# First attention of a four-stage transformer kernel: the row maxima are turned through the weighted sum's PSUM bank and spread by VectorE

## The reference, cut to what matters

```
q, k, v = split_heads(lat @ Wq, kv_input @ Wkv)      # 16 heads of 64; kv_input = [context | latents]
dots = jnp.einsum('bhid,bhjd->bhij', q, k) * scale
attn = jax.nn.softmax(dots, axis=-1)
out = jnp.einsum('bhij,bhjd->bhid', attn, v)
x = x + out.transpose(0, 2, 1, 3).reshape(b, m, heads * dim_head) @ Wout
```

## Time and profile before

| | |
|---|---|
| median of 3 runs | 777.03 us (776.41 to 777.33) |
| the profiled execution | 778.1 us, of which the span of the trace is 776.2 |
| PE busy | 694.8 us, 90% of the span |
| VectorE busy | 472.0 us, 61% |
| ScalarE busy | 394.4 us, 51% |
| GpSimd busy | 378.5 us, 49% |
| granted TensorE clock, mean | 0.955 |

### The profile page before, as it was taken

How to read it: one execution, slowest core, us unless ns; L and a number is a source line. 1 busy time by engine, 2 the same in 40 slices (tenths; PEclk the granted TensorE clock), 3 DMA queues, 4 the chain that set the end, 5 groups by cost and what they waited for, 6 DMA issues and landing times. The chain is left out here.

```text
span 776.2 us, 13776 instructions
## 1 busy us (share of the span) xinstructions
PE 694.8 (90%) x4714; PEld 421.3 (54%) x4714; DVE 472.0 (61%) x966; ACT 394.4 (51%) x676; POOL 378.5 (49%) x362
## 2 busy tenths in 40 slices
PE   4899999999999999999999999997899378559991
PEld 3654555545556546545545545557799134336661
DVE  4735474775776676578468558475343459856553
ACT  4575664564655555555465464434464255234440
POOL 7164373464454565543475455444333403766552
PEclk9999999999999999999999999999999599659997
DMA  9999999999000000000030003310210700123325
GB/s 247 182 185 185 177 188 107 3 4 4 1 1 1 2 15 1 1 1 2 2 122 2 1 1 81 124 45 12 73 43 25 223 2 11 46 69 90 85 64 179
DMA packets 109866, 50.60 MB, mean 65 GB/s; under 512 B 44804, under 2 KB 103048, under 8 KB 109800
## 3 DMA queue, kind: packets, MB, share of 16 engines
q1 hardware_dynamic: 106280, 42.46, 40.7%
q0 software_dynamic: 3520, 7.27, 2.8%
HBM read 20.07 MB, written 29.64 MB: 64 GB/s over the span
## 5 line engine op out<-in xcount | busy, mean ns | idle before, releaser
L873 ACT ACTIVATE PT<-PSUM 128x1024 f32<-128x1024 f32 x128 | 128.7, 1025 | 131.4 <-PE PSUM L1636 131.1
L692 POOL TENSOR_TENSOR PSUMS<-PT 128x1024 f32<-128x1024 f32 x32 | 76.1, 2377 | 204.8 <-ACT PT L873 166.2
L692 POOL TENSOR_TENSOR PSUMS<-PSUMS,PT 128x1024 f32<-128x1024 f32 x62 | 150.5, 2427 | 16.7 <-ACT PT L873 9.8
L1261 DVE TENSOR_REDUCE TOPS<-PSUM 128x2 f32<-128x1024 f32 x128 | 151.5, 1219 | 7.6 <-PE PSUM L1605 7.0
L1668 PE MATMUL PSUM<-PT,BIG 128*64 128x512 f32 x512 | 130.6, 611 | 0.0
L1216 DVE TENSOR_TENSOR SIL<-SIL,PSUM 128x256 f32<-128x256 f32 (+1 forms) x62 | 32.2, 519 | 61.7 <-ACT SIL L785 61.7
L1251 DVE TENSOR_TENSOR KL<-PSUM,KH 128x512 fp32r<-128x512 f32 x32 | 22.1, 690 | 68.8 <-ACT KH L846 68.6
L1605 PE MATMUL PSUM<-KH,QH 64*128 64x512 f32 x256 | 58.5, 454 | 2.6 <-DVE QL L1254 2.6
L785 ACT ACTIVATE SIL<-PSUM 128x256 f32<-128x256 f32 (+1 forms) x62 | 28.7, 463 | 57.7 <-PE PSUM L1470 34.7
L1668 PEld LDWEIGHTS PSUM<-PT,BIG 128*64 128x64 f32 x512 | 28.4, 135 | 53.0 <-issue 51.6
L1605 PEld LDWEIGHTS PSUM<-KH,QH 64*128 64x128 f32 x256 | 24.4, 185 | 58.3 <-DVE TOPS L1261 24.7
(11 more groups left out here) (257 smaller groups left out, 1347.2 us busy)
## 6 DMA issues: line engine op xcount, KB each, us to landing
lists_d<-EMPTY SPq DMA_DIRECT2D x3, 2730.0 KB, 39.5
lists_b<-EMPTY SPq DMA_DIRECT2D x3, 2470.0 KB, 35.0
lists_d<-EMPTY SPq DMA_DIRECT2D x1, 2665.0 KB, 37.0
XG<-lists_d SPq DMA_DIRECT2D x39, 65.0 KB, 1.9
lists_b<-EMPTY SPq DMA_DIRECT2D x1, 2405.0 KB, 18.0
BIG<-in_L_ffn_w SPq DMA_DIRECT2D x1, 2048.0 KB, 8.5
W2ALL<-in_L_ffn_w SPq DMA_DIRECT2D x4, 512.0 KB, 6.3
PT<-results_d SPq DMA_DIRECT2D x8, 256.0 KB, 4.8
```

The lines of the kernel that those rows point to most:

```text
L692: pool.tensor_tensor(PSUMS[:, i % 2], PTT[:, i % 2, 0] if kt == 1 else PSUMS[:, i % 2], PTT[:, i % 2, kt], ALU.add).then_inc(s_ps, 1)
L873: act.activation(PTT[:, i % 2, kt], PSUM[:, place:place + 2, :], ACT.Exp, scale=DH ** -0.5).then_inc(s_exp, 1)
L1261: dve.tensor_reduce(TOPS[:, c, 0, :], PSUM[:, place:place + 2, :], AX.X, ALU.max).then_inc(s_max, 1)
```

## The change

The turned maxima go to bank 6, `mt` is no taker any more (so the round robin shifts for all steps behind it), VectorE's reduction becomes a step of its own (`row_max`, `rm`) ahead of `P0`, and the four ScalarE copies become one VectorE product, in VectorE's queue at the place of `mt`, that is ahead of `O1`.

```diff
-        TAKES_BANKS = {"values", "context_values", "qk", "top", "max_turn", "scores", ...}
+        TAKES_BANKS = {"values", "context_values", "qk", "top", "scores", ...}
...
-            "E A B PC CA0 C CA1 O0 ADD CS V qk p0 p1 t0 s0 t1 p2 t2 D s1 t3 p3 t4 P0 P2 s2 s3 rows mt O1 OUT "
+            "E A B PC CA0 C CA1 O0 ADD CS V qk p0 p1 t0 s0 t1 p2 t2 D s1 t3 p3 t4 rm P0 P2 s2 s3 rows mt O1 OUT "
...
-        order += first_top[4:] + [("max_turn", 0), ("context_kept", 1), ("counters", 0)]
+        order += first_top[4:] + [("row_max", 0), ("context_kept", 1), ("max_turn", 0), ("counters", 0)]
...
# ScalarE
-                elif name == "max_turn":
-                    act.wait_ge(s_topt, a + 1)
-                    if a >= GROUP:
-                        act.wait_ge(s_sc, context_of(a // GROUP - 1))
-                    if a == 0:
-                        act.wait_ge(*CONST.at(0, "own"))
-                    for t in range(TPB):
-                        last = act.activation(TOPROW[:, a % GROUP, t * P:(t + 1) * P], PSUM[:, place, 0:P], ACT.Copy,
-                                              scale=OWN_TILE[:, t:t + 1])
-                    last.then_inc(s_toprow, 1)
...
# VectorE
-                elif name == "max_turn":
+                elif name == "row_max":
                     dve.wait_ge(s_max, TOPS_OF * (a + 1))
...
+                elif name == "max_turn":
+                    dve.wait_ge(s_topt, a + 1)
+                    if a == 0:
+                        dve.wait_ge(*CONST.at(0, "own"))
+                    if a >= GROUP:
+                        dve.wait_ge(s_sc, context_of(a // GROUP - 1))
+                    dve.tensor_tensor(TOPROW[:, a % GROUP, :].rearrange("p (t n) -> p t n", t=TPB),
+                                      PSUM[:, 6, 0:P].unsqueeze(1).broadcast_to([P, TPB, P]),
+                                      OWN_TILE[:, :].unsqueeze(2).broadcast_to([P, TPB, P]), ALU.mult).then_inc(s_toprow, 1)
...
# TensorE
                 elif name == "max_turn":
                     pe.wait_ge(s_comb, a + 1)
-                    pe.transpose(PSUM[:, place, 0:P], TOPT[:, :], IDENT[:, :]).then_inc(s_topt, 1)
-                    release(mine, (s_toprow, a + 1))
+                    claim(6)
+                    pe.transpose(PSUM[:, 6, 0:P], TOPT[:, :], IDENT[:, :]).then_inc(s_topt, 1)
+                    free[6] = s_toprow, a + 1
...
                         pe.wait_ge(s_v, (b + 1) * KT)
-                        if i:
-                            free[6] = s_ot, i
                         claim(6)
```

More of the change, by code:

```diff
@@ L313, in build @@
         s_cadd = sem("c_added")
-        TAKES_BANKS = {"values", "context_values", "qk", "top", "max_turn", "scores", "context_scores", "context_sums", "spread", "out", "a_turn", "r0_turn", "r0_logits", "r0_run"}
+        TAKES_BANKS = {"values", "context_values", "qk", "top", "scores", "context_scores", "context_sums", "spread", "out", "a_turn", "r0_turn", "r0_logits", "r0_run"}
         ITERATION = (
-            "E A B PC CA0 C CA1 O0 ADD CS V qk p0 p1 t0 s0 t1 p2 t2 D s1 t3 p3 t4 P0 P2 s2 s3 rows mt O1 OUT "
+            "E A B PC CA0 C CA1 O0 ADD CS V qk p0 p1 t0 s0 t1 p2 t2 D s1 t3 p3 t4 rm P0 P2 s2 s3 rows mt O1 OUT "
             "O2 O3").split()
@@ L378, in build @@
                     order.append(("scores", (i, int(at[1]))))
-                elif at in ("qk", "mt") and i + 1 < ALL:
-                    order.append(("qk" if at == "qk" else "max_turn", i + 1))
+                elif at in ("qk", "rm", "mt") and i + 1 < ALL:
+                    order.append(({"qk": "qk", "rm": "row_max", "mt": "max_turn"}[at], i + 1))
                 elif at[0] == "t" and i + 1 < ALL:
```

## The result

The changed kernel took 795.43 us (median of 4 runs, 793.12 to 797.65) beside 777.18 us for the kernel before on the same chip: ratio 1.0229, 95% interval 1.0191 to 1.0266. It is slower, as forecast, but by 18 us and not by 11: 788.3 us had been predicted, with a range up to 792.0. Run again in another comparison it took 791.71 us (6 runs, 1.0191, 1.0158 to 1.0224). The ten executions lie between 791.37 and 797.65. The profiled one took 795.24 us with a span of 793.5, against 778.1 and 776.2 before.

The account below looks back on a forecast made before the run. TensorE, busy 90% of the span, was taken as the bound, so only its waits count. 6.1 + 1.15 + 1.6 + 3.6 + 1.2 - 0.84 - 1.1 - 0.5 = +11.3 on the median 777.03 gave 788.3 us; range 781.9 to 792.

Parts of the forecast that it names:

- The reciprocals' delay: Seven iterations: three reciprocals queue behind the product; in iteration 9 they end 3.54 us after the turn starts, before 1.26.
- L1287 held by GpSimd: VectorE product with two SBUF inputs, held by GpSimd's additions; iterations 9, 17 and 25 lose 2.03 each, 6.1 us.
- the cast in iterations 16 and 24: Router slot step on VectorE, held by GpSimd's second addition until 5.23 us after the turn starts; +1.8 twice, 3.6 us.
- the exponential at the loop's end: Last group's context sums, banks 2 and 3, wait for exponentials of s3 ending at 506.64: +1.2 us.
- the table's row of predicted steps: Extra time per loop iteration, turn to turn: from 0.43 to 2.03 in nine iterations, -2.4 in the others, loop 10.1 us.
- iteration 30: Step behind the turn of iteration 29, with the router's steps between L1287 and KL: +0.78 us.
- The gains: TOPROW waits gone in iterations 5, 13, 21 (0.84), seven plain iterations of 0.16 (1.1), context sums (0.5): 2.4 us.
- the 0.5 for the context sums: A smaller gap ahead of the context sums, estimated at 0.07 in seven iterations: gain of 0.5 us.
- the rivals: L1287 and slots unheld: 781.9 (0.12); only slots unheld: 784.7 (0.12); reciprocals' delay hidden: 774.6 (0.03); product held: 820 (0.04).

Follow-up runs that it names:

- all mended: Changed kernel with reciprocals ahead of the product, slot steps ahead of the turn, first turn through bank 7, last context sums in banks 0 and 1: 775.11 us, 0.9965.
- the two with the bank only: Kernel before with the turn in bank 6, no taker, ScalarE's copies kept: 779.41 us; same with first turn in bank 7, last context sums in banks 0, 1: 777.76.
- reciprocals first: Changed kernel with the three late reciprocals put ahead of the turn and product again in VectorE's queue: 781.29 us, 1.0051.
- one fill: Changed kernel with one matmul of zeros ahead of the waiting top t0 in iteration 26 alone: 794.55 us, 1.0225.
- other banks: Changed kernel with the first turn through bank 7 and the last group's first context sums in banks 0 and 1: 791.37 us, 1.0188.
- product only: Changed kernel with VectorE's product and order, but the turn again a taker of banks 0 to 5 as before: 790.66 us, 1.016.
- short third addition: Changed kernel with GpSimd's third addition of key tiles cut to 8 of 512 columns a head, for timing only: 783.71 us, 1.0075.
- slots first: Changed kernel with the router's slot steps put ahead of P0 and the turn, in the iteration before: 791.71 us, 1.0179.
- short fills: Changed kernel with one matmul of zeros ahead of each of five waiting tops, in iterations 10, 16, 18, 24 and 26: 791.29 us, 1.0174.
- the bank only with the other banks: Kernel before with the turn in bank 6 and no taker, first turn through bank 7, last context sums in banks 0 and 1: 777.76 us, 1.0000.

## Why the prediction was right and wrong

**Right: the direction, and each stall by its place.** The reciprocals' delay, L1287 held by GpSimd, the cast in iterations 16 and 24, the exponential at the loop's end: every one stands in the profile where it was put. Without the falls of the clock the table's row of predicted steps differs from the measured ones by 0.04 to 0.1 us each, except iteration 30 (1.02 for 0.78). There the prediction took the two additions as one stretch of 4.9 us; in the trace the second began 0.44 us behind the end of the first, and L1286, held to its end, took 1.78 us instead of the 1.50 of iteration 13. The gains were 2.1 and not 2.4: three times 0.25, and six plain iterations with 0.22 where seven with 0.16 had been put down, but nothing of the 0.5 for the context sums. The loop was predicted 10.1 us longer; without the falls it is 11.2.

**Right: the rivals were turned down for the right reason.** The Trainium skill (SBUF — State Buffer, section "SBUF: two separate sides") names a lock between GpSimd and VectorE. The prices measured here were: L1286 1.47 us behind a full addition and 0.69 behind a short one, the cast 2.24, and the product of one PSUM and one SBUF input 690 to 693 ns in all 32 cases, though additions run beside it. The trace agrees with that page.

**Wrong: the sum had no term for the granted clock.** The prediction costed each wait by its own length. Behind two of the new waits TensorE then ran for some 4 us at or near the 1.2 GHz level, which added 1.6 us each: 14.3 us in the loop instead of 11.2. The price is shown, by the windows and by the same iterations without a fall in other kernels (1.90 for 3.50, 2.08 for 3.62). That the waits bring the falls is argued from where they stand, behind waits each time; no run isolates it. It is the largest single part of the miss.

**Wrong: the start.** That `claim(6)` makes the first turn wait for the copy of the context's keys was missed, though the line is in the diff: +0.6 (1.42 us for 0.8). The experiment with bank 7 took that wait away.

**The account.** From profile to profile the span grew by 17.3 us: 1.0 at the start (0.6 of it the wait), 14.3 in the loop, 1.2 at its end, and 0.7 behind it. Against the predicted 11.3 (its terms, as printed, add up to 11.2) that is 6.0 too much: 3.1 falls of the clock, 1.1 in the terms of the loop, 1.0 at the start, 0.7 behind, which no experiment followed up. The remaining 1.1 up to the median's miss of 7.1 us is the choice of executions: the profiled one of the kernel before lay 1.1 us above its median. The medians of two comparisons of the changed kernel, 795.43 and 791.71, lie 3.7 us apart, more than any of these terms. By the second the range would have held, by luck, for its upper end, 792.0, left no room for the falls or the start.

**What stays open** is which waits bring a fall, and whether it is they that do. Every fall seen in the loop followed a wait or a cluster of them, and none was seen in the loops without the long ones (before, all mended, the two with the bank only). But the same wait of 1.9 us in iteration 16 was followed by a fall in three traces (the changed kernel twice, reciprocals first) and by none in two others (one fill, other banks), nor in product only, where it was 1.65 us. In iteration 24 the same wait was followed by none in any of these six. The short third addition keeps t0's waits and had no fall, and the fall in iteration 10 appeared once. That the unaltered kernel repeated both its falls speaks against mere chance; what else decides, the runs don't tell.

The Trainium skill (TensorE: Matmul & The Clock Gate, section "What's actually happening") says that the chip judges TensorE's activity on a schedule that runs freely and doesn't start with the kernel, by which the same wait could be caught in one place and missed in another. No run here measures that schedule.

## What to carry to other kernels

A step that waits for another engine should not be put ahead of ready work in an in-order queue: the four ScalarE copies cost TensorE 2.0 us of waits in all where they stood, and a product that takes 0.69 us for their 1.14 cost up to 14 us because three reciprocals and a cast queued behind it. When an edit brings waits of one or two microseconds on TensorE, cost them with and without a fall of its clock behind each, and put that into the range. And when a resource is shared anew (bank 6), look up who holds it at the first and the last use, not only in the steady loop: two of this change's costs sit there.

## What the runs showed of the hardware that was not expected

**The clock behind short waits.** In a loop in which TensorE is otherwise busy, one wait of 1.9 us can be followed by a granted clock of 0.50, which stays down for some 4 to 8 us, by windows of 2 us, though TensorE is fully busy. It can also stay up. The price was 1.5 to 1.6 us in most cases, 0.8 behind the first turn of one fill, and 2.9 in iteration 10 of slots first.

**The rise at the start of the third stage, and why medians wander.** The second stage ends at the 1.2 GHz level in every trace. The rise comes at different points: windows of 7 us at the same distance behind the last turn, first of the changed kernel run again, then with short fills.

```profile
630.00:637.00 7.00, 4.71 (x18) 0.50 0.97 264
637.00:644.00 7.00, 5.68 (x58) 0.88 0.00 0
644.00:651.00 7.00, 4.72 (x62) 1.00 0.01 2
```

```profile
626.00:633.00 7.00, 4.64 (x18) 0.50 1.03 286
633.00:640.00 7.00, 6.22 (x46) 0.50 0.01 2
640.00:647.00 7.00, 5.33 (x56) 0.74 0.01 2
```

The time from the last turn to the end of the span is 287.4 us in the first and 291.0 in the second. The three traces with a window of 0.50 there (short fills, reciprocals first, slots first) needed 288.4 to 291.0 us, while the changed kernel in its two traces needed 287.1 and 287.4 and product only, which rose first, 282.9. The rise is not the whole of it: the bank only with the other banks rose late too (0.57 in that window) and needed 285.6, and of the 3.4 us by which all mended is longer there (288.6 against 285.2 before), 2.3 were lost within 35 us behind the last turn, 0.3 at the first context sums and the rest at the wait for XG and the fall behind it. So this stretch, which the change touches only at its start, differs by more than the gain of the best version: all mended gave back 3.4 of the 4.6 us that it had won up to the last turn. Hence the loop was judged by its steps, not by the medians.

**Zeros are not cheap.** A float32 matmul of 128x512 with zero weights stands in the trace as two, and takes 1.13 us for one and 2.84 for three, while the 128x512 matmuls of `qk` start 0.23 us apart.
